# Two tiles to a step of TensorE in a gathering convolution

## The chip, the cores and the metric

The program runs on one core of one Trainium2 chip. The time is that of the device for one execution, in microseconds (us); lower is better. TensorE multiplies matrices and writes into the banks of PSUM, ScalarE and VectorE read and write them, GpSimd (POOL) and SyncE (SP) do the rest, SP issues nearly all transfers.

## The reference

The network has 16 sequences of 512 tokens with 128 channels. Its first half is a convolution with learnt positions: every token and each of 8 heads has a frequency and a phase, from which come 32 sampling positions, and at each a linear interpolation between two tokens and a weight out of 64 bins.

```
pos  = clip(l + phase + freq * (taps), 0, L - 1)
g    = x[floor(pos)] + frac(pos) * (x[floor(pos) + 1] - x[floor(pos)])
w    = kmat[bin(freq, phase, tap)]            # (x @ kernel_w.T + kernel_b)
y    = sum over taps of w * g                 # then y @ out_w.T
x    = x + ga * y
```

Its second half is a mixture of 8 experts, two of them for each token, with `silu(h1) * h2` between two products, and a residual.

## The kernel before

**Tiles.** Two sequences are a pair (`PAIRS` = 8; called a batch pair below where it could be confused). Tokens are taken by their remainder r modulo 8 (`RES` = 8), a row R is one remainder of a pair, and a tile T is one head h of a row: 8 x 8 x 8 = 512 tiles of 128 x 512. A tile counts how many taps lie beyond each gap between tokens. For each:

- `gap_on(T)` (L981): TensorE multiplies 32 rows of parameters with `cp` into PSUM bank T modulo 4 (`BANKS`), after VectorE has emptied that bank (`s_aw`).
- `gap(T)` (L769): ScalarE takes Relu of the bank in place, scaled (L775).
- `tile_on(T)` (L987) and `undone_on(T)` (L992): TensorE adds two more products to the bank, of the same 32 parameters with the two halves of `cn`. The first waits for the Relu (`s_e`).
- `weighted(T)` (L1290): VectorE takes the maximum with a constant and multiplies by weights, from PSUM into `aw[T % RING]` (L1303).
- `turn_tile(T)` (L996): TensorE turns the tile, four 128 x 128 transposes (L1000), into one of the two banks `ps_t`.
- `tile_evicted(T)` (L777): ScalarE copies it into `att` (L783).
- `weigh(R, g)` (L1010): 32 products of 128 x 32 weights (L1020) sum four heads.

The parameters of tile T stand on the partitions 32 (T modulo 4) to 32 (T modulo 4) + 31 (`strip`, L976), so that products of neighbouring tiles use different strips of 32 rows of the array.

**The order.** Each engine has its list written out. In step T TensorE does `undone_on(T + 1)`, `tile_on(T + 2)`, `gap_on(T + 3)`, `turn_tile(T)`, and then what belongs to the head: at h = 0 the counts of the next row (L973), at 1 the second weighing of the row before, at 2 and 4 the turns of the edge terms (L1007), at 3 the bins of a later row (L946), at 5 the first weighing, at 7 the edge weighing (L1030). In some rows there are more: turns of the normed input (r = 2) and output (r = 3), of parameters (4, 5) and steps (6) at h = 6 and 7, the products of the waves (3), scores (4) and ranks (5) at h = 0, and the output products (L1042) at h = 6 of row 0 and h = 0 of row 6.

The two banks `ps_t` are given out in the order of the list ORDER, in turn, to everything that TensorE turns: tiles, counts, edges and the rest. TensorE waits before each:

```
    if u >= 2:
        pe.wait_ge(s_ev, u - 1)      # unit(), L897: unit u - 2 is evicted
    return ps_t[u % 2]
```

ScalarE does in step T `gap(T + 3)`, `tile_evicted(T)`, then the eviction of the counts (L767), of edges (L790), the copy of the row (`copied`, L798, h = 3), and in rows 1 and 2, at h = 1 and 3, `centred` (L735, four slices each). VectorE does `weighted(T)` and then edge terms, bins and norms. SP stores and loads the rows' weights and edges through DRAM, ahead by one or two rows.

After the 512 tiles come the choice of experts and their 135 blocks of tokens.

Of the kernel before, what the change touches and what calls it, by code (L numbers as in the profile page):

```python
# [13 lines left out]
NT = PAIRS * TILES  # L14
# [5 lines left out]
ROWS = 32  # L20
QUAD = P // ROWS
KRING = 4
RING = 3
BANKS = 4
SCALE = 2.0 ** 27
GATE = 2.0 ** 90
# [64 lines left out]
def build(nc, x, wave_wT, wave_b, kern_wT, kern_b, out_wT, w12T, w3T, gateT, cT, wmod,  # L91
# [23 lines left out]
    with ctx:  # L115
# [58 lines left out]
        ee = sb("ee", [P, 2, 512])  # L174
        aw = sb("aw", [P, RING, 512])
        att = sb("att", [P, SLOTS, 512])
# [532 lines left out]
        def _(act):  # L709
# [59 lines left out]
            def gap(T):  # L769

                i, r, h = T // TILES, T // HEADS % RES, T % HEADS
                act.wait_ge(s_p, T + 1)
                if T % TILES == 0:
                    act.wait_ge(s_par, i + 1)
                act.activation(ps_s[T % BANKS][:, :], ps_s[T % BANKS][:, :], ACT.Relu, scale=f27[:, i % 2, r, h:h + 1]).then_inc(s_e, 1)  # L775
# [27 lines left out]
            for n in range(4):  # L803
                params_turned(0, n)
            counted(0)
            for T in range(BANKS - 1):
                gap(T)
            for b in range(2):
                steps_turned(0, b)
            for T in range(NT):  # L810
                i, R, r, h = T // TILES, T // HEADS, T // HEADS % RES, T % HEADS
                last, more = i - 1, i + 1 < PAIRS
                if T + BANKS - 1 < NT:
                    gap(T + BANKS - 1)
                tile_evicted(T)
                if h == 0 and R + 1 < NR:
                    counted(R + 1)
                if h == 2:
                    edge_evicted(R, 0)
                if h == 3 and R:  # L820
                    copied(R - 1)
                if h == 4:
                    edge_evicted(R, 1)
                if i:
                    if (r, h) in ((2, 1), (2, 3)):
                        centred(1, last, h // 2)
                    if r == 3 and h >= 6:
                        h2_turned(last, h - 6)
                    if (r, h) == (4, 5):
                        gap_tanh(last)  # L830
                if more:
                    if (r, h) in ((1, 1), (1, 3)):
                        centred(0, i + 1, h // 2)
                    if r == 2 and h >= 6:
                        h_turned(i + 1, h - 6)
                    if (r, h) == (3, 3):
                        waves(i + 1)
                    if r == 4 and h >= 6:
                        params_turned(i + 1, h - 6)
                    if r == 5 and h >= 6:  # L840
                        params_turned(i + 1, h - 4)
                    if r == 6 and h >= 6:
                        steps_turned(i + 1, h - 6)
# [34 lines left out]
        def _(pe):  # L878
# [102 lines left out]
            def gap_on(T):  # L981
                if T >= BANKS:
                    pe.wait_ge(s_aw, T - BANKS + 1)
                at, params = strip(T)
                nc.tensor.matmul(ps_s[T % BANKS][:, :], params, cp[at, :], start=True, stop=True).then_inc(s_p, 1)  # L985

            def tile_on(T):  # L987
                pe.wait_ge(s_e, T + 1)
                at, params = strip(T)
                nc.tensor.matmul(ps_s[T % BANKS][:, :], params, cn[at, 0, :], start=False, stop=False, skip_group_check=True)  # L990

            def undone_on(T):  # L992
                at, params = strip(T)
                nc.tensor.matmul(ps_s[T % BANKS][:, :], params, cn[at, 1, :], start=False, stop=True, skip_group_check=True).then_inc(s_n, 1)  # L994
# [75 lines left out]
            for n in range(4):  # L1070
                params_turned(0, n)
            counts(0)
            for T in range(BANKS - 1):
                gap_on(T)
            tile_on(0)
            undone_on(0)
            tile_on(1)
            for b in range(2):
                steps_turned(0, b)
            for T in range(NT):  # L1080
                i, R, r, h = T // TILES, T // HEADS, T // HEADS % RES, T % HEADS
                last, more = i - 1, i + 1 < PAIRS
                if T + 1 < NT:
                    undone_on(T + 1)
                if T + 2 < NT:
                    tile_on(T + 2)
                if T + BANKS - 1 < NT:
                    gap_on(T + BANKS - 1)
                turn_tile(T)
                if h == 0 and R + 1 < NR:  # L1090
                    counts(R + 1)
                if h == 1 and R:
                    weigh(R - 1, 1)
                if h == 2:
                    turn_edges(R, 0)
                if h == 3 and R + 2 < NR:
                    bins(R + 2)
                if h == 4:
                    turn_edges(R, 1)
                if h == 5:  # L1100
                    weigh(R, 0)
                if h == 7:
                    weigh_edges(R, 0)
                    weigh_edges(R, 1)
                if i:
                    if (r, h) == (0, 6):
                        outputs(last, 1)
                    if r == 3 and h >= 6:
                        h2_turned(last, h - 6)
                    if (r, h) == (4, 0):  # L1110
                        scores(last)
                    if (r, h) == (5, 0):
                        ranks(last)
                if more:
                    if r == 2 and h >= 6:
                        h_turned(i + 1, h - 6)
                    if (r, h) == (3, 0):
                        waves(i + 1)
                    if r == 4 and h >= 6:
                        params_turned(i + 1, h - 6)  # L1120
                    if r == 5 and h >= 6:
                        params_turned(i + 1, h - 4)
                    if r == 6 and h >= 6:
                        steps_turned(i + 1, h - 6)
                if (r, h) == (6, 0):
                    outputs(i, 0)
# [55 lines left out]
        def _(dve):  # L1182
# [107 lines left out]
            def weighted(T):  # L1290
# [5 lines left out]
                dve.wait_ge(s_n, T + 1)  # L1296
                if T >= RING:
                    dve.wait_ge(s_at, UNIT["tile", T - RING] + 1)
# [8 lines left out]
            def edge_terms(R):  # L1307

                dve.wait_ge(s_ev, UNIT["count", R] + 1)
                dve.wait_ge(s_kd, R + 1)  # L1310
                if R >= 2:
                    dve.wait_ge(s_est[R % 2], 32 * (R // 2))
                nc.vector.scalar_tensor_tensor(kr[:, R % 2, :], en[:, R % 2, :], -TAPS / 2 * SCALE, kd[:, R % 2, :], ALU.add, ALU.mult).then_inc(s_kr, 1)
# [38 lines left out]
            binned(0)  # L1352
            binned(1)
            edge_terms(0)
            for T in range(NT):
                i, R, r, h = T // TILES, T // HEADS, T // HEADS % RES, T % HEADS
                last, more = i - 1, i + 1 < PAIRS
                weighted(T)
                if h == 2 and R + 1 < NR:
                    edge_terms(R + 1)  # L1360
                if h == 5 and R + 2 < NR:
                    binned(R + 2)
                if more:
                    if (r, h) == (0, 1):
                        first_spread(i + 1, 0)
                    if (r, h) == (0, 3):
                        first_spread(i + 1, 1)
                    if (r, h) == (0, 4):
                        deviation(0, s_rs1)
                    if (r, h) == (3, 2):  # L1370
                        waves(i + 1)
                    if (r, h) == (3, 6):
                        periods(i + 1)
                if i:
                    if (r, h) == (1, 0):
                        new_x(last, 1)
                    if (r, h) == (1, 3):
                        second_spread(last, 1)
                    if (r, h) == (1, 4):
                        deviation(1, s_rs2)  # L1380
                    if (r, h) == (4, 2):
                        scores(last)
                    if (r, h) == (4, 4):
                        choices(last)
                    if (r, h) == (4, 5):
                        masks(last)
                    if (r, h) == (5, 2):
                        ranks_read(last)
                    if (r, h) == (5, 3):
                        spotted(last, 0)  # L1390
                    if (r, h) == (5, 4):
                        spotted(last, 1)
                if (r, h) == (6, 2):
                    new_x(i, 0)
                if (r, h) == (7, 5):
                    second_spread(i, 0)
# [161 lines left out]
```

## Time and profile before

| | us |
|---|---|
| median of 3 runs | 1334.32 |
| lowest, highest | 1331.52, 1336.67 |
| profiled execution | 1336.08 |
| its span | 1334.0 |
| TensorE busy (share of the span) | 1141.6 (86%) |
| ScalarE | 916.3 (69%) |
| VectorE | 702.3 (53%) |
| GpSimd | 588.1 (44%) |
| granted TensorE clock, mean | 0.956 |

The page divides the span in 40 slices; the tiles run from 37 us to the slices near 970 us. PE is TensorE's matmuls and PEld its weight loads, which can run beside them; DVE is VectorE, ACT is ScalarE. L with a number is a line of the kernel.

### The profile page before, as it was taken

What the parts mean: (1) busy time and instruction counts of PE and PEld (TensorE: products, weight loads), DVE (VectorE), ACT (ScalarE), POOL (GpSimd) and SP (SyncE); (2) the same over time, 40 slices, a digit from 0 to 9 for tenths busy, and PEclk for the clock granted to TensorE, in tenths of its full rate; (3) what the DMA queues carried; (4) which work ended last, traced back from release to release, by engine and by line L of the source; (5) the groups of instructions that cost most, each with busy time, mean ns of one, the idle gap of its engine ahead of it and who ended that gap; (6) DMA issues with size and microseconds to landing.
All of it is one profiled execution on the core that took longest, in us unless ns stands there. A gap on an engine that the chain in (4) does not pass through costs nothing. (4 is left out here: it accounts for less than half of the span.)

```text
span 1334.0 us, 34820 instructions
## 1 busy us (share of the span) xinstructions
PE 1141.6 (86%) x11855; PEld 741.1 (56%) x11855; DVE 702.3 (53%) x2252; ACT 916.3 (69%) x1906; POOL 588.1 (44%) x838
## 2 busy tenths in 40 slices
PE   5699999999999999999999999999922989999840
PEld 2366656656665665666566566656621656556520
DVE  4345655564665656566565656556551333333336
ACT  2488887888888788878878888887700555555520
POOL 4133155346436435633643563442436554545520
PEclk9899999999999999999999999999955999999975
DMA  5546446445645544554554455444412442222237
GB/s 181 156 123 175 112 144 162 136 134 165 156 124 167 163 125 140 168 144 121 168 162 127 143 151 138 143 140 116 150 64 68 138 133 72 71 71 71 68 138 262
DMA packets 213178, 179.81 MB, mean 135 GB/s; under 512 B 147600, under 2 KB 183184, under 8 KB 212368
## 3 DMA queue, kind: packets, MB, share of 16 engines
q1 hardware_dynamic: 204336, 159.68, 42.5%
q0 software_dynamic: 8672, 17.92, 4.1%
q8 instruction: 100, 1.64, 0.5%
q14 instruction: 70, 0.57, 0.2%
HBM read 95.42 MB, written 82.12 MB: 133 GB/s over the span
## 5 line engine op out<-in xcount | busy, mean ns | idle before, releaser
L1303 DVE SCALAR_TENSOR_TENSOR aw<-ps,ks 128x64 f32<-128x64 f32 (+7 forms) x960 | 382.0, 437 | 387.4 <-PE ps L994 342.8
L775 ACT ACTIVATE ps<-ps,f 128x512 f32<-128x512 f32 x512 | 343.4, 671 | 131.2 <-PE ps L985 131.2
L1000 PE MATMUL ps<-ident,aw 128*128 128x128 f32 x2048 | 332.9, 285 | 31.6 <-ACT att L783 15.9
L783 ACT ACTIVATE att<-ps 128x512 f32<-128x512 f32 x512 | 310.2, 606 | 11.5 <-PE ps L1000 11.2
L1000 PEld LDWEIGHTS ps<-ident,aw 128*128 128x128 f32 x2048 | 216.3, 141 | 157.9 <-issue 134.4
L604 POOL COPY kn<-kn 128x256 f32<-128x256 f32 x64 | 25.4, 397 | 436.8 <-DVE kn L1287 436.8
L990 PE MATMUL ps<-cn,ptt 32*128 32x512 bf16 x512 | 198.8, 388 | 13.9 <-ACT ps L775 13.9
L994 PE MATMUL ps<-cn,ptt 32*128 32x512 bf16 x512 | 198.7, 388 | 0.0
L985 PE MATMUL ps<-cp,ptt 32*128 32x512 bf16 x512 | 197.9, 389 | 0.0
L705 POOL DMA_INDIRECT y_scratch<-aw,idu x135 | 129.3, 958 | 129.4 <-ACT aw L866 128.1
L853 ACT ACTIVATE ee<-ps 128x256 f32<-128x256 f32 x135 | 51.9, 385 | 152.8 <-PE ps L1144 152.8
L573 POOL DMA_INDIRECT slot_scratch<-hrow,spotu x128 | 127.3, 995 | 48.2 <-issue 33.4
L1144 PE MATMUL ps<-kn,ee 128*128 x270 | 143.0, 612 | 0.0
L1020 PE MATMUL ps<-att,dl 128*32 128x128 f32 x4096 | 140.0, 278 | 0.1
L1450 DVE TENSOR_TENSOR aw<-ee,ps 128x256 f32<-128x256 f32 x135 | 56.9, 421 | 136.4 <-ACT ee L853 135.5
L1020 PEld LDWEIGHTS ps<-att,dl 128*32 128x32 f32 x4096 | 105.1, 110 | 22.2 <-ACT att L790 10.6
L994 PEld LDWEIGHTS ps<-cn,ptt 32*128 32x128 bf16 x512 | 46.4, 91 | 124.6 <-issue 121.2
L1138 PE MATMUL ps<-ident,dl 128*128 128x128 f32 x135 | 38.3, 283 | 55.0 <-DMA dl<-slot_scratch 32.7
L1007 PE MATMUL ps<-ident,ka 128*128 128x128 f32 x512 | 77.3, 274 | 7.8 <-POOL ka L617 7.8
L790 ACT ACTIVATE att<-ps 128x512 f32<-128x512 f32 x128 | 77.9, 608 | 8.3 <-PE ps L1007 8.3
L1159 PE MATMUL ps<-hgr,aw 128*128 x540 | 82.5, 275 | 0.1
L1151 PEld LDWEIGHTS ps<-ident,aw 128*128 128x128 f32 x270 | 38.0, 141 | 71.6 <-issue 46.4
(176 smaller groups left out, 1652.1 us busy)
## 6 DMA issues: line engine op xcount, KB each, us to landing
k_scratch<-kn SPq DMA_DIRECT2D x64, 512.0 KB, 3.5
ka<-e_scratch SPq DMA_DIRECT2D x64, 512.0 KB, 3.2
ks<-k_scratch SPq DMA_DIRECT2D x128, 130.0 KB, 3.3
e_scratch<-kr SPq DMA_DIRECT2D x128, 126.0 KB, 3.4
dl<-slot_scratch SPq DMA_DIRECT2D x135, 65.0 KB, 1.8
att<-y_scratch SPq DMA_DIRECT2D x16, 512.0 KB, 5.2
xc<-in_x SPq DMA_DIRECT2D x8, 512.0 KB, 5.9
h_scratch<-hx SPq DMA_DIRECT2D x16, 256.0 KB, 4.2
```

Of the source, the lines that this page charges most:

```text
L573: pool.indirect_dma_start(out=slots[:, :], out_offset=bass.IndirectOffsetOnAxis(ap=spotu[:, k * RES + r:k * RES + r + 1], axis=0), in_=hro ...
L705: pool.indirect_dma_start(out=yscr[:, :], out_offset=bass.IndirectOffsetOnAxis(ap=idu[:, s:s + 1], axis=0), in_=yrow[:, y, :], in_offset=N ...
L775: act.activation(ps_s[T % BANKS][:, :], ps_s[T % BANKS][:, :], ACT.Relu, scale=f27[:, i % 2, r, h:h + 1]).then_inc(s_e, 1)
L783: act.activation(att[:, h, :], ps_t[UNIT["tile", T] % 2][:, :], ACT.Copy).then_inc(s_ev, 1)
L985: nc.tensor.matmul(ps_s[T % BANKS][:, :], params, cp[at, :], start=True, stop=True).then_inc(s_p, 1)
L990: nc.tensor.matmul(ps_s[T % BANKS][:, :], params, cn[at, 0, :], start=False, stop=False, skip_group_check=True)
L994: nc.tensor.matmul(ps_s[T % BANKS][:, :], params, cn[at, 1, :], start=False, stop=True, skip_group_check=True).then_inc(s_n, 1)
L1000: last = nc.tensor.transpose(bank[:, j * P:j * P + P], aw[:, T % RING, j * P:j * P + P], ident[:, :])
L1020: last = nc.tensor.matmul(ps_y[ROWS * k:ROWS * k + ROWS, g * P:g * P + P], dl[:, R // RES % 2, j, h, :], att[:, h, j * P:j * P + P], start ...
L1144: nc.tensor.matmul(ps_h[j % 2][:, :], xT[:, j % 2, :], w12[:, bass.ds(experts[j % 8] * (2 * FF), 2 * FF)], start=True, stop=True).then_inc ...
L1159: last = nc.tensor.matmul(ps_z[j % 2][:, 0:C], hidT[:, j % 2, k * P:k * P + P], w3[:, bass.ds(experts[j % 8] * (HALVES * C) + k * C, C)], ...
L1303: ins = nc.vector.scalar_tensor_tensor(dst[:, a:b, :], src[:, a:b, :], -TAPS * SCALE, rows(ks[:, R % 2, h, o:o + 1], [[0, b - a], [1, HP]] ...
```

## The change

RING goes from 3 to 4. TensorE's list is rewritten for pairs of tiles: at each even T it does `tile_on` of T + 2 and T + 3, `gap_on` of T + 4 and T + 5, `undone_on` of T + 2 and T + 3, and then `turn_tile(T)`; at odd T only `turn_tile(T)`; what belongs to each head follows its turn as before. ScalarE does both `gap(T + 4)` and `gap(T + 5)` ahead of `tile_evicted(T)` at even T, and none at odd T. VectorE weights tile T + 2 in step T. ORDER and its banks stay.

```diff
-RING = 3
+RING = 4
@@ ScalarE
-            for T in range(BANKS - 1):
+            for T in range(BANKS):
                 gap(T)
...
-                if T + BANKS - 1 < NT:
-                    gap(T + BANKS - 1)
+                if h % 2 == 0 and T + BANKS < NT:
+                    gap(T + BANKS)
+                    gap(T + BANKS + 1)
                 tile_evicted(T)
@@ TensorE
-            for T in range(BANKS - 1):
+            for T in range(BANKS):
                 gap_on(T)
-            tile_on(0)
-            undone_on(0)
-            tile_on(1)
+            for T in range(2):
+                tile_on(T)
+            for T in range(2):
+                undone_on(T)
...
-                if T + 1 < NT:
-                    undone_on(T + 1)
-                if T + 2 < NT:
+                if h % 2 == 0 and T + 2 < NT:
                     tile_on(T + 2)
-                if T + BANKS - 1 < NT:
-                    gap_on(T + BANKS - 1)
+                    tile_on(T + 3)
+                    if T + BANKS < NT:
+                        gap_on(T + BANKS)
+                        gap_on(T + BANKS + 1)
+                    undone_on(T + 2)
+                    undone_on(T + 3)
                 turn_tile(T)
@@ VectorE
+            for T in range(2):
+                weighted(T)
             for T in range(NT):
...
-                weighted(T)
+                if T + 2 < NT:
+                    weighted(T + 2)
```

## Rows read from the trace of the kernel before

**Rows 1.** Busy us of each engine in a stretch, granted clock, DMA share, GB/s.
```profile
168.00:936.00 768.00, 731.01 (x8785) 477.07 (x8784) 454.73 (x1436) 641.99 (x1247) 361.84 (x547) 1.00 0.52 145
```

**Rows 2.** Waits: engine line, what ended them: us, times, longest.
```profile
ACT ps L775 <- PE ps L985: 131.2, 210, 1.8
...
PEld ps L1000 <- issue: 134.4, 476, 0.5
...
PEld ps L994 <- issue: 121.2, 462, 1.5
...
PE ps L1000 <- ACT att L783: 15.9, 75, 0.2
```

**Rows 3.** Timeline of a pair A: start us, us, engine line, what [idle before].
```profile
536.61 0.38 PE L990 MATMUL ps<-cn,ptt 32*128 32x512 bf16 x1
...
536.92 0.42 PEld L1000 LDWEIGHTS ps<-ident,aw 128*128 128x128 f32 x4 [0.23 <-issue]
...
537.02 0.76 DVE L1303 SCALAR_TENSOR_TENSOR aw<-ps,ks 128x128 f32<-128x128 f32 x2 [0.97 <-PE ps L994]
537.07 0.66 ACT L775 ACTIVATE ps<-ps,f 128x512 f32<-128x512 f32 x1 [0.37 <-PE ps L985]
...
537.42 0.38 PE L973 MATMUL ps<-ce,ptt 128*128 128x252 bf16 x2
...
537.65 0.59 ACT L783 ACTIVATE att<-ps 128x512 f32<-128x512 f32 x1
...
538.13 0.59 ACT L767 ACTIVATE en<-ps 128x504 int32<-128x504 f32 x1
...
538.36 0.42 PEld L1000 LDWEIGHTS ps<-ident,aw 128*128 128x128 f32 x4 [0.48 <-issue]
...
539.17 0.62 ACT L783 ACTIVATE att<-ps 128x512 f32<-128x512 f32 x1
...
539.65 1.66 ACT L735 ACTIVATE hrow<-xo,shift,rstd 128x128 f32<-128x128 f32 x4
...
539.96 0.39 PE L990 MATMUL ps<-cn,ptt 32*128 32x512 bf16 x1
```

**Rows 4.** Timeline of a pair B and the pair C behind it.
```profile
510.96 0.38 PE L990 MATMUL ps<-cn,ptt 32*128 32x512 bf16 x1
...
512.71 0.42 PEld L1000 LDWEIGHTS ps<-ident,aw 128*128 128x128 f32 x4 [0.31 <-issue]
...
514.16 0.39 PE L990 MATMUL ps<-cn,ptt 32*128 32x512 bf16 x1
...
515.91 0.42 PEld L1000 LDWEIGHTS ps<-ident,aw 128*128 128x128 f32 x4 [0.31 <-issue]
...
517.52 0.38 PE L990 MATMUL ps<-cn,ptt 32*128 32x512 bf16 x1
```

**Rows 5.** Timeline of a pair D with no unit, up to the first line of rows 3.
```profile
533.91 0.38 PE L990 MATMUL ps<-cn,ptt 32*128 32x512 bf16 x1
...
535.40 0.42 PEld L1000 LDWEIGHTS ps<-ident,aw 128*128 128x128 f32 x4 [0.23 <-issue]
...
535.99 0.44 PEld L1030 LDWEIGHTS ps<-att,hgr 128*32 128x32 f32 x16 [0.17 <-issue]
```

**Rows 6.** Timeline of a pair D with units: its strips, second turns, next strips.
```profile
548.51 0.39 PE L990 MATMUL ps<-cn,ptt 32*128 32x512 bf16 x1
...
550.25 0.42 PEld L1000 LDWEIGHTS ps<-ident,aw 128*128 128x128 f32 x4 [0.31 <-issue]
...
552.04 0.09 PEld L990 LDWEIGHTS ps<-cn,ptt 32*128 32x128 bf16 x1
```

**Rows 7.** Timeline: wave products, weighing at the lower clock, turns behind VectorE.
```profile
553.07 1.86 PE L939 MATMUL ps<-ww,ht 128*128 128x16 f32 x16
...
570.94 1.94 PE L1020 MATMUL ps<-att,dl 128*32 128x128 f32 x32
...
580.83 0.66 PE L1000 MATMUL ps<-ident,aw 128*128 128x128 f32 x4 [0.77 <-DVE aw L1303]
```

## The prediction

> **What bounds the kernel now.** I read the busy time by stage first. In the stage that holds 425 of the 512 tiles [rows 1] TensorE is busy 731 of 768 us and ScalarE 642, with the clock granted in full (1.00, which is the 2.4 GHz level). TensorE's matmul ends are modelled, so that figure doesn't say that it is saturated; the waits do more [rows 2]: ScalarE waits 131 us for a gap product, TensorE waits for an eviction 75 times, and TensorE's weight loads stand 121 us (462 times) before the strip products and 134 us (476 times) before the turns for no other engine. Those last two are what the change is aimed at. The timeline shows how a step runs. I write a time as the distance from the start S of the strip products.
>
> A row of eight heads is four pairs of tiles: A (h 0, 1), with the counts between its turns and the first weighing last; B (2, 3), with edge turns between and the bins last; C (4, 5), edge turns between and a weighing last; D (6, 7), with the edge weighing last and in some rows a further unit of turns behind each tile. Pair A before [rows 3]: strips 536.61, turns' loads 536.92 (+0.31, taken 0.32), counts 537.42 (0.50 later). ScalarE starts Relu of the gap at +0.46, the eviction of tile 0 at +1.04 and the counts' at +1.52; its rows are 0.66 and 0.59 long, but they follow each other by 0.58 and 0.48, so these are the spacings to add. The next step's strips are short, yet the second tile's turns are loaded only at 538.36 (+1.75), 0.12 after the eviction of tile 0 ends (537.65 + 0.59). The cause is in the code: there are two banks for turns, each taken by every second unit of ORDER. With counts or edges between, tile T+1 needs the bank of tile T. From those loads to the next strips it is 1.60 (539.96 - 538.36). The pair takes 3.35, and ScalarE's chain sets it.
>
> **The change, part by part.**
> *ScalarE's order.* In a pair ScalarE now does gap, gap, eviction instead of gap, eviction, gap, eviction. Both gap products are issued in the strip phase at S, so the first Relu still starts at +0.46; the second starts at 1.03, the eviction of tile T at 1.61, and it ends at 2.20. The turns of T+1, if something else has used the other bank, load at 2.32. That is one Relu, 0.57, later than in pair A before. TensorE waits in order, and the weighing or bins and all the next strips are behind the waiting turns. The next gap products are among these, so ScalarE idles then and the delay comes again each pair.
>
> *TensorE's phases.* The fourth strip product has a strip and bank of its own, as the three before it. No row shows four; I take it as free, between 0 and one product, 0.39. The two second products stand behind their tiles' first on the same strips, which the rows don't show either: between 0 (wholly beside) and 0.39 after them. I take 0.20. A phase before the turns then takes 0.52 (bounds 0.32 and 0.9) where there were two of 0.32. A move from turns into strips costs 0.08 more than on to the next turns or counts (0.59 from 535.40 to the edge weighing at 535.99 [rows 5], 0.50 in [rows 3]). So a pair that waits for nobody saves 0.32 + 0.32 + 0.08 - 0.52 = 0.20.
>
> The pairs after the change:
> - A: 2.32 + 1.60 = 3.92, against 3.35: +0.57. Its turns of T start at 0.52 and are done for ScalarE 0.81 later (538.36 to 539.17 [rows 3]), at 1.33, before the 1.61 at which it comes to them; the counts end near 1.3. All of TensorE's longer phase is therefore hidden in the wait, up to a phase of 0.8; beyond it the excess is added.
> - B [rows 4]: before, 510.96 to 514.16, 3.20, not quite waiting; after, 2.32 + 1.45 (512.71 to 514.16) = 3.77: +0.57.
> - C [rows 4]: before, 514.16 to 517.52, 3.36; after, 2.32 + 1.61 (515.91 to 517.52) = 3.93: +0.57.
> - D with no unit between [rows 5]: before, 533.91 to 536.61, 2.70; after, both banks are free: 0.52 + 0.50 + 0.59 + 0.61 = 2.22: -0.48. ScalarE ends its last eviction's turn at 2.56, before the next pair's first gap at 2.68. VectorE weights two tiles from 0.62 (0.10 after the turns' loads [rows 3]) at 0.76 each, to 2.14, just in time for the gap products at 2.22.
> - D with units [rows 6]: before, 548.51 to 552.04, 3.53; after, 2.32 + 1.79 (550.25 to 552.04) = 4.11: +0.58, taken 0.57. In the row after the gates' scores, TensorE already stood 0.77 there for VectorE [rows 7], which now runs two tiles ahead: that one is taken at 0.
> - Pairs in which TensorE has other work between the turns (the 16 wave products, 1.86 us [rows 7], the scores, the outputs twice) cover ScalarE's chain: -0.20 each.
> - The rows in which ScalarE also centres four slices twice. Centring fills it for 1.54 (539.65 to the next Relu; its row is 1.66). Before, A to C of such a row took 548.51 - 536.61 = 11.90 against 3.35 + 3.20 + 3.36 = 9.91: 1.99 extra. After: the first batch runs from 3.61 to 5.15 where the next gap wants ScalarE at 4.38, 0.77 late; the second, behind the copy of the row, is about 1.33 late. Together 2.10, so 0.1 more in each of the two such rows.
>
> *VectorE's order, RING 4, the queues.* The weighted tile moves two loop steps ahead, but still waits for its second product, so in time it stays 0.1 behind the strips' end. Ahead of it nothing is lost: behind it stand the edge terms, bins and norms, with whole rows of slack to their loads. No DMA or instruction is added on SP's or POOL's queue, and their waits on weighted tiles come true earlier, not later. The fourth buffer costs nothing: 0.
>
> **The sum.** A full batch pair (64 tiles, 32 pairs): A, B and C are 24, less 3 covered, 21 x 0.57 = 12.0; D with units 4 x 0.57 = 2.3, and one at 0; plain D 2 x -0.48 = -1.0; covered 4 x -0.20 = -0.8; centring 0.2. That is +12.7. The first batch pair has no outputs, scores or h2 turns from one before it: 22 x 0.57 + 4 x 0.57 - 4 x 0.48 - 2 x 0.20 + 0.1 = +12.6. The last one has no turns for a next: 22 x 0.57 + 0.57 - 6 x 0.48 - 3 x 0.20 + 0.1 = +9.7. Together 6 x 12.7 + 12.6 + 9.7 = 98.5, of it 199 pairs at +0.57 (113 us). The experts' stage and the end are untouched: 0. The profiled execution took 1336.1 us (its span is 1334.0), so about 1434; the median of the three runs shown is 1334.3, which makes it 1432.
>
> The Trainium skill (TensorEngine Tiling, Performance Considerations, PSUM Bottleneck) says that tiling speeds up TensorE but not the evacuation of PSUM, which can become the bottleneck. The trace agrees: the wait at 538.36 ends with an eviction. The same page (Key Properties) says that a change of tiling mode drains TensorE. By that rule alone, one entry and one exit less per pair, the change would gain the 51 us of the first rival.
>
> **The rivals.**
> 1. *TensorE's own phases decide, and the kernel gets faster.* Each pair saves 0.20: 256 x 0.20 = 51 us, 1285; with second products wholly beside, 0.40 each, 1234. For it: the 255 us before strips and turns in [rows 2], and only 75 waits for evictions. Against it: it decides only if the eviction of T ends before 1.5, when the turns and the edges behind them are over, and gap, gap and eviction alone take 0.57 + 0.58 + 0.59 from 0.46. Within 0.5% of no change would need both effects to cancel.
> 2. *ScalarE's delay is partly given back.* If in half of the 199 pairs that I count at +0.57 the delay only takes up time that TensorE or VectorE loses anyway in this profile (as the 0.77 in [rows 7]), 57 us go: about 1375. Against it: pair A shows no such time.
> 3. *The strips aren't side by side.* With the fourth product and the second ones each a product's length, the phase is 1.1 rather than 0.52. ScalarE's chain moves little; some 50 uncovered pairs get 0.6 longer, and the rest up to 0.3 where the phase passes 0.8: +30 to +90, from 1462 on.
> 4. *TensorE's clock falls, with more standing still.* At the lower level of 1.2 GHz the 32 weighing products took 1.94 [rows 7], where the 1.60 of [rows 3], less 0.59 for four turns [rows 5], leave 1.01. If half of the 128 weighings ran so, 64 x 0.93 = 60 more: 1492. Against it: the wait per pair is 0.8 us, and the stage is granted 1.00 with waits of 0.7 to 1.1 in it.
>
> **Chances.** The forecast's case 0.73, rival 1 0.06, no change 0.03, rival 2 0.06, rival 3 0.08, rival 4 0.04. About 0.5% is what can be told from no change here. Faster 0.06, same 0.03, slower 0.91. The forecast's own bounds: a phase of 0.32 instead of 0.52 takes 0.2 from some 45 pairs (-9), one of 0.9 adds 20; the spacings are good to 0.05, 200 times (10 either way). With parts of rivals 2 and 3: 1400 to 1468.
>
> **What would show it.** Right: in pairs A to C the strips follow each other by 3.8 to 3.9, two Relus stand next to each other on ScalarE, and the wait of turns L1000 for the eviction L783 grows from 16 us to well over 100; a plain D pair takes about 2.2; four strip products start within 0.05, the two second ones about 0.2 later; the clock stays 1.00. Wrong: turns of odd tiles that follow the counts or edges without a wait, a time under 1390, or a granted clock below 1.

## The result: slower, and what the profile after shows

| | before | changed |
|---|---|---|
| median of 4 runs, us | 1335.03 | 1422.18 |
| lowest, highest | 1331.52, 1336.67 | 1419.76, 1424.6 |
| profiled execution, its span | 1336.08, 1334.0 | 1419.76, 1417.9 |

The ratio is 1.0651, 95% interval 1.0633 to 1.0669: 87 us slower, inside the range, 10 under the forecast of 1432.

The stage of the tiles answers to [rows 1]: busy us of each engine (PE, PEld, DVE, ACT, POOL), granted clock, DMA share, GB/s. TensorE and ScalarE are both less busy, 626 and 602 of 768 us where they were 731 and 642. Each waits for the other. The mean granted clock of the stage stays 1.00, with one short fall in it, from about 326 to 330 us.

```profile
168.00:936.00 768.00, 625.84 (x8012) 413.58 (x8010) 399.20 (x1312) 602.15 (x1140) 335.49 (x506) 1.00 0.48 134
```

The waits of the kernel after (engine line, what ended them: us, times, longest) answer to [rows 2]. The strips' entries have halved in number, from 462 to 241 (121 us to 82); those of the turns fell from 476 to 286, at the same 134 us. But the turns now wait 181 us for the eviction L783, where it was 16. Their weight loads show 199.5 us put down to VectorE. In the pair below that can't be the last thing waited for: VectorE had weighted the second tile by 508.82, four us before its turns.

```profile
PEld ps L1001 <- DVE aw L1307: 199.5, 188, 2.1
PE ps L1001 <- ACT att L783: 180.7, 203, 1.8
...
PEld ps L1001 <- issue: 134.1, 286, 2.1
ACT ps L775 <- PE ps L986: 103.6, 163, 3.0
...
PEld ps L991 <- issue: 82.1, 241, 1.5
```

A pair B of the kernel after, in order of time (start us, us, engine line, what, idle before); it answers to the first half of [rows 4]. The strips start at 510.83, the two second products 0.23 later, the turns' loads at +0.53. The two Relus stand in one row of 1.24 us from +0.44. The eviction L783 comes at +1.59. The second turns are loaded at +2.30 (513.13), 0.11 after it ends; their products follow at 513.16. TensorE has stood 0.71 us for it, with the bins and the next strips behind. The pair takes 3.76; the forecast had 3.77 with the turns at 2.32.

```profile
510.83 0.39 PE L991 MATMUL ps<-cn,ptt 32*128 32x512 bf16 x2
...
511.06 0.38 PE L995 MATMUL ps<-cn,ptt 32*128 32x512 bf16 x2
511.27 1.24 ACT L775 ACTIVATE ps<-ps,f 128x512 f32<-128x512 f32 x2 [0.75 <-PE ps L986]
511.36 0.42 PEld L1001 LDWEIGHTS ps<-ident,aw 128*128 128x128 f32 x4 [0.42 <-issue]
...
512.42 0.60 ACT L783 ACTIVATE att<-ps 128x512 f32<-128x512 f32 x1
...
513.16 0.63 PE L1001 MATMUL ps<-ident,aw 128*128 128x128 f32 x4 [0.71 <-ACT att L783]
...
514.59 0.39 PE L991 MATMUL ps<-cn,ptt 32*128 32x512 bf16 x2
```

The same trace shows the starts of the strips at both ends of four stretches. A plain pair D takes 2.16 (423.46 to 425.62). A whole batch pair, from one h = 0 of row 0 to the next, takes 127.23 (425.62 to 552.85). The D in the row after the scores takes 3.83 (502.94 to 506.77), where it took 4.06 before. The D with units of [rows 6], forecast at 4.11, takes 4.09 (597.60 to 601.69).

```profile
423.46 0.39 PE L991 MATMUL ps<-cn,ptt 32*128 32x512 bf16 x2
425.62 0.39 PE L991 MATMUL ps<-cn,ptt 32*128 32x512 bf16 x2
...
502.94 0.39 PE L991 MATMUL ps<-cn,ptt 32*128 32x512 bf16 x2
...
506.77 0.39 PE L991 MATMUL ps<-cn,ptt 32*128 32x512 bf16 x2
...
552.85 0.39 PE L991 MATMUL ps<-cn,ptt 32*128 32x512 bf16 x2
...
597.60 0.39 PE L991 MATMUL ps<-cn,ptt 32*128 32x512 bf16 x2
...
601.69 0.39 PE L991 MATMUL ps<-cn,ptt 32*128 32x512 bf16 x2
```

A batch pair of the kernel before took 115.8 (its strips of row 0 start at 391.81 and at 507.60). So a full batch pair is 11.4 us longer, 68.5 for the six of them. The first rose by 8.8 and the last by 5.9, which makes 83 of the 84 us between the two traces.

### The profile page after: what moved, and what is told of

Same layout as the page of the kernel before. It is cut to its first block, busy times and chain, and to the rows that moved or that the text cites. A ratio compares the mean times of both kernels' runs of the same rounds, so it can differ in the third digit from the quotient of the medians.

```text
span 1417.9 us, 34825 instructions
## 1 busy us (share of the span) xinstructions
PE 1087.7 (77%) x11855; PEld 712.5 (50%) x11855; DVE 680.7 (48%) x2252; ACT 935.5 (66%) x1906; POOL 587.4 (41%) x838
## 4 chain that ended last, share of the span: by engine, by line
PE 51%; ACT 19%; issue 19%; DMA 4%; DVE 3%; POOL 3%; SPq 1%; ACTq 0%; POOLq 0%; DVEq 0%
PE ps L1001 12%; ACT att L783 10%; PE ps L1021 8%; PE ps L1148 8%; ACT ps L775 6%; PE ps L991 4%; PE ps L1163 4%; PE ps L947 3%; PE ps L1043 2%; PE ps L1031 2%; PE ps L1155 2%; DMA att<-y_scratch 2%; PE ps L1142 1%; POOL y_scratch L705 1%; ACT hrow L735 1%
## 5 line engine op out<-in xcount | busy, mean ns | idle before, releaser
L1307 DVE SCALAR_TENSOR_TENSOR aw<-ps,ks 128x64 f32<-128x64 f32 (+7 forms) x960 | 366.9, 434 | 490.6 <-PE ps L995 341.9
L1001 PE MATMUL ps<-ident,aw 128*128 128x128 f32 x2048 | 327.2, 285 | 180.7 <-ACT att L783 180.7
L1001 PEld LDWEIGHTS ps<-ident,aw 128*128 128x128 f32 x2048 | 218.1, 142 | 333.7 <-DVE aw L1307 199.5
L775 ACT ACTIVATE ps<-ps,f 128x512 f32<-128x512 f32 x512 | 317.1, 658 | 103.6 <-PE ps L986 103.6
L783 ACT ACTIVATE att<-ps 128x512 f32<-128x512 f32 x512 | 303.6, 598 | 99.8 <-PE ps L1001 99.8
L986 PE MATMUL ps<-cp,ptt 32*128 32x512 bf16 x512 | 101.6, 389 | 3.2 <-DVE aw L1307 3.0
L991 PE MATMUL ps<-cn,ptt 32*128 32x512 bf16 x512 | 100.8, 388 | 0.7 <-ACT ps L775 0.7
L995 PE MATMUL ps<-cn,ptt 32*128 32x512 bf16 x512 | 98.1, 378 | 0.0
L790 ACT ACTIVATE att<-ps 128x512 f32<-128x512 f32 x128 | 77.6, 606 | 6.3 <-PE ps L1008 6.3
L1163 PEld LDWEIGHTS ps<-hgr,aw 128*128 128x128 f32 x540 | 70.9, 191 | 0.3 <-issue 0.3
```

The lines of the kernel that those rows point to most:

```text
L783: act.activation(att[:, h, :], ps_t[UNIT["tile", T] % 2][:, :], ACT.Copy).then_inc(s_ev, 1)
L1001: last = nc.tensor.transpose(bank[:, j * P:j * P + P], aw[:, T % RING, j * P:j * P + P], ident[:, :])
L1163: last = nc.tensor.matmul(ps_z[j % 2][:, 0:C], hidT[:, j % 2, k * P:k * P + P], w3[:, bass.ds(experts[j % 8] * (HALVES * C) + k * C, C)], ...
L1307: ins = nc.vector.scalar_tensor_tensor(dst[:, a:b, :], src[:, a:b, :], -TAPS * SCALE, rows(ks[:, R % 2, h, o:o + 1], [[0, b - a], [1, HP]] ...
```

## The experiments

The runs came in three groups, each on a chip of its own with runs of the kernel before beside them. The first group is e1, e2, e4 and e5, the second c1, e1b, e6 and e7, the third e3, e7b and e8. On the first two chips the kernel before took 1407 and 1404 us; on the third, 1334. Traces of the first two groups show two things more than those of a quiet chip. One is stops of about 2 us, after which ScalarE or VectorE, often both within 0.1 us, start again on work that TensorE had finished; a pair of 3.91 then takes 5.79. The lines below are of e4_half_relu, where the second product L995 was over at 437.4. The other is more falls of the granted clock: between 60 and 926 us these traces have 5 to 25 of them, where those at 1334 us for the kernel before have 0 to 6. The changed kernel itself has 14 in c1_after_again, with 55 us at the lower level, and 1 in the first trace, with 3.4 us.

```profile
439.76 1.03 ACT L775 ACTIVATE ps<-ps,f 128x512 f32<-128x512 f32 x2 [1.61 <-remote]
439.83 0.76 DVE L1307 SCALAR_TENSOR_TENSOR aw<-ps,ks 128x64 f32<-128x64 f32 x2 [4.08 <-remote]
```

So totals are compared as ratios to the kernel before of the same group, and the lengths of single pairs are read where no stop and no fall of the clock lies in them. No trace of the kernel before was taken on those two chips, so how stops and falls share its 70 us isn't shown.

### Theory and rivals

The theory is that of the forecast: at even T two Relus stand ahead of the eviction of tile T on ScalarE, the second turns of the pair need that tile's bank, and everything of TensorE is queued behind them. One rival: the grouping of TensorE's work costs by itself. The other: the order of the units costs alike in both kernels. A unit is whatever takes a bank `ps_t` besides the tiles: counts, edges and the further turns of rows 2 to 6.

**e1_evict_between** and again **e1b_evict_between**, beside the changed kernel in **c1_after_again**.

```diff
                 if h % 2 == 0 and T + BANKS < NT:
                     gap(T + BANKS)
-                    gap(T + BANKS + 1)
                 tile_evicted(T)
+                if h % 2 == 0 and T + BANKS < NT:
+                    gap(T + BANKS + 1)
```

> Base: the changed kernel (1422). ScalarE does gap(T+4), the eviction of tile T, gap(T+5) at even T in place of gap, gap, eviction; all other engines keep their lists. Theory (one Relu more stands ahead of the eviction that the turns of T+1 need): the eviction can start when the first turns are done, 0.53 + 0.81 = 1.34 after the strips in place of 1.61, so the second turns load 0.27 earlier in some 200 pairs, 54 less; plain D pairs wait some 0.3 for the second Relu instead, 8 more: about 1376 (1365 to 1390). The wait of the turns L1001 for the eviction falls from 181 us to about 120. Rival (TensorE's grouping itself is the price: two products deep on one strip, or pairs that drain longer): ScalarE's order is no matter, 1422 within 7.

> The changed kernel once more, as the reference for the runs beside it. On the chip of the last four runs the kernel before took 1407 in place of 1335, with stops of 1.5 to 4 us of ScalarE and VectorE at once strewn through the tiles, so the changed kernel has to be seen beside them. Theory: ratio to the kernel before 1.065 on a quiet chip; where such stops add the same to both, 1.06. Rival (the stops hide part of the wait): under 1.05.

> The same kernel as e1_evict_between, now beside the changed kernel: ScalarE does gap, eviction, gap at even T. In the trace of e1 the pairs A and C took 3.7 and 3.6, B 3.4 to 3.5. Theory: some 200 pairs get 0.2 to 0.37 shorter than in the changed kernel, 45 to 65 us less (ratio to the kernel before 1.02 to 1.03 where that of the changed kernel is 1.065). Rival (ScalarE's order is no matter): as c1_after_again within 7 us.

Measured: e1 1407.15 us, ratio 1.0011 (0.9986 to 1.0036). In the second group the changed kernel took 1485.96, ratio 1.0578 (1.0513 to 1.0643), and e1b 1413.44, 1.0057 (1.0025 to 1.0088). ScalarE's order alone gives back 73 us (10 either way), nearly all of the loss, with every list of TensorE left as the change made it. That is more than the 45 to 65 expected. Most pairs A, B and C are 0.36 to 0.37 shorter, which for 199 pairs would be 73 us; c1's trace also has five falls of the clock more than e1b's, at about 1.5 us each. The trace of e1b shows a pair C (404.14 to 407.68, 3.54, where the changed kernel has 3.91): the first turns' loads come at +0.53, the eviction starts 0.70 later and not 0.81, and the second turns load at +1.94. The 0.81 of the expectation came from a row in which ScalarE was itself busy until then. The wait for the eviction went from 167 us in c1 to 109.

```profile
404.14 0.39 PE L992 MATMUL ps<-cn,ptt 32*128 32x512 bf16 x2
...
404.58 0.66 ACT L775 ACTIVATE ps<-ps,f 128x512 f32<-128x512 f32 x1 [0.17 <-PE ps L987]
404.67 0.42 PEld L1002 LDWEIGHTS ps<-ident,aw 128*128 128x128 f32 x4 [0.42 <-issue]
...
405.37 0.60 ACT L783 ACTIVATE att<-ps 128x512 f32<-128x512 f32 x1
...
406.11 0.63 PE L1002 MATMUL ps<-ident,aw 128*128 128x128 f32 x4 [0.34 <-ACT att L783]
```

The first rival falls as the cause of the loss: the same grouping with ScalarE's order changed is within 0.6% of the kernel before.

**e4_half_relu** takes a part of the suspected cost away (it leaves out the Relu of half the columns of the odd tiles), **e6_extra_op** adds to it.

```diff
-                act.activation(ps_s[T % BANKS][:, :], ps_s[T % BANKS][:, :], ACT.Relu, ...
+                act.activation(ps_s[T % BANKS][:, 0:512 >> T % 2], ps_s[T % BANKS][:, 0:512 >> T % 2], ACT.Relu, ...
```

> Base: the changed kernel. The Relu of the odd tiles works on 256 of their 512 columns; the other half of the columns stays without it, so the tiles' values differ. Nothing else changes. Theory: a 256-column operation of ScalarE takes about 0.2 less than one of 512 (the copy L798 0.39 to 0.42 against 0.60), the second Relu of a pair stands in the chain ahead of the eviction, and each of some 200 waiting pairs gets shorter by that 0.2: 1382 (1374 to 1390). Rival (ScalarE has slack, it is busy 78% of the stage): under 5 us.

Measured: 1433.92, ratio 1.018 (1.0118 to 1.0242); the changed kernel has 1.058, but in the second group and on another chip, so some 55 us less, 12 either way. Pairs A, B and C take 3.69, 3.54 and 3.69 where they are undisturbed, 0.22 less each, as expected. The total can't be told from their 199 x 0.22 = 44, though it lies below the range that was written down.

```diff
                     gap(T + BANKS + 1)
+                if h % 2 == 0:
+                    if T:
+                        act.wait_ge(s_extra, T // 2)
+                    act.activation(unused[:, :], kw[:, :], ACT.Copy).then_inc(s_extra, 1)
                 tile_evicted(T)
```

> Base: the changed kernel. ScalarE does one more operation at each even T, a copy of 128x512 from SBUF into a tile that nobody reads, between the second Relu and the eviction of tile T. Theory: it stands in the chain, 0.5 each: 199 waiting pairs x 0.5, plus the two dozen plain D pairs, which become ScalarE's: 112 more than c1_after_again (95 to 130), for ScalarE work of 256 x 0.5 = 128. Rival (ScalarE is idle for a fifth of the stage and has room for it): under 30 more.

Measured: 1605.72, ratio 1.143 (1.138 to 1.1481), 120 us over c1_after_again for 256 operations of 0.5, where 112 was expected. Undisturbed pairs B and C take 4.28 and 4.42, 0.5 more each; the trace also has seven falls of the clock more than c1's. In the lines below (e6, a pair C that ends at 502.90) the extra row L821 stands between Relu and eviction, and TensorE stands 1.23 us. In the changed kernel ScalarE has a fifth of the stage free (602 of 768 us busy), and still it passes on nearly all that is put ahead of the eviction.

```profile
500.07 0.63 ACT L821 ACTIVATE unused<-kw 128x512 f32<-128x512 f32 x1
500.59 0.60 ACT L785 ACTIVATE att<-ps 128x512 f32<-128x512 f32 x1
...
501.33 0.63 PE L1007 MATMUL ps<-ident,aw 128*128 128x128 f32 x4 [1.23 <-DVE aw L1313]
```

That wait is put down to VectorE here, which by the program's order weights the tiles of the next pair at that time; the turns' loads (501.30) come 0.11 after the eviction ends, as in the others.

**e2_units_last** takes away what makes the second turns wait, the unit between; **e5_before_units_last** does the same to the kernel before.

```diff
-                if h == 0 and R + 1 < NR:
-                    counts(R + 1)
                 if h == 1 and R:
                     weigh(R - 1, 1)
-                if h == 2:
-                    turn_edges(R, 0)
+                if h == 1 and R + 1 < NR:
+                    counts(R + 1)
                 if h == 3 and R + 2 < NR:
                     bins(R + 2)
-                if h == 4:
-                    turn_edges(R, 1)
+                if h == 3:
+                    turn_edges(R, 0)
                 if h == 5:
                     weigh(R, 0)
+                    turn_edges(R, 1)
```

ORDER and ScalarE's list follow.

> Base: the changed kernel. The counts go from behind turn T to behind the weighing of h = 1, the edge turns from h = 2 and 4 to behind the bins of h = 3 and the weighing of h = 5, in ORDER, on TensorE and on ScalarE (their evictions last in these steps, behind the centring). So the second turns of a pair take the bank that nobody waits for. Theory: the wait for the eviction goes, the pairs A, B, C take about 3.0, 3.05 and 3.2 in place of 3.9, 3.76 and 3.9; where other products stood between the turns it saves nothing (+0.2), in the centring rows ScalarE bounds: 8 batches x 13.6 less, about 1313 (1295 to 1335), faster than the kernel before. Rival (grouping is the price): the pairs keep most of their length, 1400 or more.

> Base: the kernel before, with the same move of counts and edge turns as in e2_units_last, so one tile to a step. Theory: before, only pair A waited for the eviction (0.3), B and C were as long as TensorE's own work; A saves 0.2, B and C lose 0.05 by one more switch each: 1325 to 1340, no change or just faster. So the move is worth something only where two Relus stand ahead of the eviction. Rival (the order of units is what costs in both kernels): a gain like that of e2, 60 us or more.

Measured: e2 1376.3, ratio 0.9778 (0.9733 to 0.9823), where 1313 of 1334, 0.984, was expected and 0.97 to 1.00 was the range: a fast kernel out of the slow one, again with the strips' grouping untouched. e5 1515.29, ratio 1.0785 (1.0737 to 1.0834): a miss, I had expected no change. The waits of e5 tell why: ScalarE takes its list in order and stands for the edge turns that now come last (96 us), the next Relu is late behind them, and with one tile to a step TensorE's next strips wait for that Relu, 90 us (27 in the kernel before). In the paired kernel the Relus lead by a whole pair, and the same stand of ScalarE (54 us in e2) costs little. Undisturbed pairs B of e5 take 3.95 and more where it was 3.20, apart from the rows that centre, and pairs C 3.82 where it was 3.36. The trace of e5 also has 25 falls of the clock with 92 us at the lower level, so a part of its 108 us is the clock's. These are lines of e5.

```profile
ACT att L790 <- PE ps L1007: 95.9, 108, 6.3
PEld ps L990 <- ACT ps L775: 90.4, 173, 2.5
```

So the second rival falls too: the late units help the kernel whose gap products are a pair ahead, and cost the other.

**e7_all_last**, twice, puts the further units of rows 2 to 6 behind both turns as well.

```diff
-                    if r == 3 and h >= 6:
-                        h2_turned(last, h - 6)
+                    if (r, h) == (3, 7):
+                        for n in range(2):
+                            h2_turned(last, n)
```

and so for the other units, in ORDER and on both engines.

> Base: e2_units_last (counts and edge turns last in their pair). Here the two further units of turns in rows 2 to 6 go behind the edge weighing of h = 7 too, so that no pair has a unit between its two turns of tiles. Theory: a D pair with units takes 3.4 in place of 4.1, 35 pairs, 25 us less than e2, whose ratio to the kernel before was 0.978: 0.96 (0.95 to 0.97), faster than both kernels. Rival (ScalarE then stands for the units that come last, as it did 54 us for the edges in e2): 0.975 or more.

> e7_all_last once more, as the reference beside e8: ratio to the kernel before 0.968 as before (0.96 to 0.975).

Measured: 1360.83, ratio 0.9681 (0.963 to 0.9733), inside its range, and on the chip without stops 1306.42 against 1334.2, ratio 0.9791 (0.9778 to 0.9805). That one is a miss: 0.96 to 0.975 was expected, and it lies where e7's rival put it. The D pairs of rows 2 to 6 did get 0.75 shorter than in e2 (4.24 to 3.49, 3.99 to 3.22). But the pair A behind them in row 5 takes 3.81, where e2 has 3.16; TensorE stands 0.57 us there for VectorE. How much the rival's reason, ScalarE standing for the late units, has in it isn't shown, as e2 wasn't run on this chip. Still e7b beats both kernels: 28 us under the one before, and 116 us under the changed kernel's 1422.18. A pair C of e7b and the D with units behind it: eight turns in one go at +0.53, no wait, the edge turns last; 3.16 where it was 3.36 before and 3.91 in the changed kernel. The D takes 3.22 (3.28 for the one of the same row before, 3.83 changed). Not every pair gains: B of rows 3 to 6 takes 3.7 to 4.1, where it was 3.20.

```profile
459.73 0.39 PE L997 MATMUL ps<-cn,ptt 32*128 32x512 bf16 x2
...
460.26 0.86 PEld L1007 LDWEIGHTS ps<-ident,aw 128*128 128x128 f32 x8 [0.42 <-issue]
...
461.29 1.08 PE L1027 MATMUL ps<-att,dl 128*32 128x128 f32 x32
...
462.30 0.42 PEld L1014 LDWEIGHTS ps<-ident,ka 128*128 128x128 f32 x4 [0.20 <-issue]
...
462.89 0.39 PE L997 MATMUL ps<-cn,ptt 32*128 32x512 bf16 x2
...
466.11 0.39 PE L997 MATMUL ps<-cn,ptt 32*128 32x512 bf16 x2
```

**e8_all_last_between** is e7 with the edit of e1.

> Base: e7_all_last, with ScalarE's order of e1 (gap, eviction, gap at even T). Theory (the order matters only through the bank that the second turns wait for): here no second turn of a pair takes the bank of the first, so the order that gave 73 us in e1 gives nothing, within 10 us of e7; the plain D pairs may lose 0.3 each where TensorE comes to the second Relu too early. Rival (gap, eviction, gap is better for ScalarE by itself): 40 to 70 us less than e7, a ratio to the kernel before near 0.92.

Measured: 1310.21, ratio 0.9823 (0.9809 to 0.9836), 4 us slower than e7b beside it, within the 10 expected. The order that gave 73 us gives nothing once no second turns take the bank of the first. This ties the loss to the bank, and not to ScalarE's order as such.

**e3_ring3** has `RING = 3`.

> Base: the changed kernel with RING back at 3, so the weighted tile T+2 waits for the turns of T-1 and T+3 for those of T. Theory: both are over long before VectorE comes there (0.6 and 1.4 us after the strips), no change against the changed kernel, a ratio to the kernel before of 1.05 to 1.065. Rival (the fourth buffer carries the pair): VectorE waits for the first turns, and the ratio passes 1.07.

Measured: 1426.57, ratio 1.0685 (1.0669 to 1.0701). The ratio lies 0.0035 above the range of the expectation and below the rival's 1.07. An undisturbed batch pair takes 127.22, as with four buffers, and every kind of pair is as long as it was. Four of the six full batch pairs take 128.4 to 130.3: the trace has six falls of the granted clock between 60 and 926 us, with 20 us at the lower level, against one with 3.4 us in the changed kernel's. That makes 6.8 of the 7.3 us between the two traces. Whether three buffers bring the falls or only this execution had them isn't shown; the mean clock of the changed kernel's own four runs goes from 0.944 to 0.963, that of e3's four from 0.940 to 0.957.

## Why the prediction was right

**ScalarE's order** was the step that decided, and it held by its own numbers: second turns at 2.30 (2.32 forecast), A, B and C at 3.91, 3.76 and 3.91 (3.92, 3.77, 3.93). e1b, e4 and e6 move that chain by -0.37, -0.22 and +0.5 a pair and the time follows each; e8 shows that it acts through the bank.

**TensorE's phases** held: four strip products start within 0.01, the second ones 0.23 later (0.20 taken between 0 and 0.39), the phase is 0.53 (0.52). A plain D takes 2.16 (2.22), as nobody waits for ScalarE there. The prediction's 0.20 a pair, for one entry to the strips and one exit less, was right in sign and a little small. Of the 0.54 that the plain D saved, 0.27 is a wait for the Relu that the kernel before had: its second strips stood from 534.82 to 535.09. That leaves 0.27. Rival 1's saving is real in these pairs.

```profile
534.81 0.09 PEld L994 LDWEIGHTS ps<-cn,ptt 32*128 32x128 bf16 x1 [0.17 <-issue]
...
535.08 0.09 PEld L990 LDWEIGHTS ps<-cn,ptt 32*128 32x128 bf16 x1 [0.18 <-ACT ps L775]
```

**The sum** was 98 us, and 87 came by the medians, 84 between the traces. The mechanism was right, and its terms were a little too large, nearly all in the same direction. By full batch pair, of the 12.7 forecast 11.4 came. Against a batch pair of before without a clock drop, the B and C of the two centring rows rose by 1.75 us in all, where 4 x 0.57 + 0.2 = 2.48 was counted. There the centring makes the pair longer by 0.73 and 1.13 in the one row and by 0.65 and 1.09 in the other, not by 0.77 and 1.33. The other waiting pairs A, B and C rose by 0.54 to 0.58, 0.28 less in all than by 0.57 each. The D pair after the scores got 0.23 shorter, not 0: there the unit is of bf16 turns, and the wait for VectorE went. The D with units and the plain D came out 0.09 and 0.10 under their terms. The covered pairs gave back 0.62, not 0.8, which goes the other way.

In the first batch pair 8.8 came of the 12.6 forecast. Its pair B of row 0 holds a stand of some 10 us in both kernels (13.35 before, 11.50 after), and the kernel before had a lower clock there (0.80 from 36 to 61, against 1.00 from 36 to 60). In the last 5.9 came of 9.7: the kernel before lost 1.5 us there to a fall of the clock, and four pairs of the last two rows, where the bins and then the counts are missing, rose by 0.6 in all, where the sum has 2.3. None of this was in the sum. It took a further 7.7 us off, in the same direction as the other terms, so the total isn't close by errors that cancel.

**VectorE's lead, RING and the queues** were taken at 0. e3 agrees for RING in the undisturbed pairs. Nothing was run for VectorE's lead or the queues by themselves.

**The rivals.** Rival 2 didn't come: the waiting pairs rose by 0.54 to 0.58 each, and only the D after the scores hid the delay. Rival 3 falls by the 0.23. Rival 4 came once, and small: the mean clock of the stage stayed 1.00 through waits of 0.7 us a pair and more. But behind a wait of 1.8 us for the eviction, in a row that centres (322.8 to 324.6), the clock fell for 3.4 us, and that batch pair took 128.7, not 127.2. The prediction's sign of being wrong, a granted clock below 1, was drawn too sharply: the kernel before had two such falls.

The Trainium skill (TensorEngine Tiling, Performance Considerations, PSUM Bottleneck) warns that tiling doesn't speed up the copy out of PSUM, which may become the bottleneck. The traces agree that the loss lies at such a copy, the eviction L783, with a point added by e1b and e8: it is its place in ScalarE's list that counted, at 78% busy, and not its rate. The same page (Key Properties) says that a change of tiling mode drains TensorE. The plain D pair agrees: 0.27 shorter, beyond the wait that it lost, with one entry and exit less.

## What to carry to other kernels

When work is grouped to save an engine's switches, write down for each buffer that two engines share which instruction frees it, and what the freeing engine has ahead of that instruction in its list. An operation moved ahead of the release adds nearly its whole length to every group that waits for it, though the engine has idle time left. Put units that share a ring of two banks so that a group's own members take different banks, with the odd one last. And if a wait is moved to the end of a group, the next group's inputs should be a group ahead, as e5 against e2 shows.

## What the runs showed of the hardware

- Products on the same strip of 32 rows, the second accumulating on the first, started 0.23 us apart (510.83 and 511.06) at a granted clock of 1.00, though a row of 32x512 is 0.38 long; on different strips they start within 0.01 of each other. So here the row's length was not the price of the next product on its strip.
- Two chips ran the same kernel before at 1404 to 1407 us against 1334 on a third. Their traces show stops of about 2 us, after which ScalarE or VectorE, often both, start again, and 5 to 25 falls of the granted clock, against 0 to 6. What the stops wait for stays open; "remote" is all that the traces give.
- In the kernel before the granted clock fell twice in the stage shown, about 570 to 574 and 914 to 919, and the batch pair with the first took 117.3 against 115.8. TensorE had been at work for the whole of the 2 us before the first fall (first line), and was so while the clock stood near its lower level, 0.5 (0.55 and 0.60 are means of 2 us). In the changed kernel it fell once, and there TensorE had stood 1.84 us shortly before. Columns as above.

```profile
568.00:570.00 2.00, 2.00 (x20) 1.77 (x18) 0.06 (x1) 1.13 (x3) 1.85 (x5) 1.00 0.73 169
570.00:572.00 2.00, 2.00 (x27) 1.59 (x28) 1.84 (x8) 1.26 (x2) 1.07 (x1) 0.55 0.89 160
572.00:574.00 2.00, 2.00 (x28) 1.15 (x17) 0.92 (x9) 0.50 (x1) 0.00 (x0) 0.60 0.49 94
```
